# A loop over batch rows, written out for all 16 rows

## What is computed

```python
# attention: each block of 128 queries sees its own, the block before and the block after,
# and within these only keys at a distance of at most 128
scores = einsum('bhnqd,bhnkd->bhnqk', qb, kwin) / 16      # masked to -1e30
out = einsum('bhnqk,bhnkd->bhnqd', softmax(scores), vwin) @ Wout + bout
x = layernorm(x + out)
# FFN with both weight matrices quantised to -1, 0, 1
h = relu(x @ Wq1.T + b1)
x = layernorm(x + h @ Wq2.T + b2)
```

## Time and profile before

| | |
|---|---|
| three runs | 1191.0, 1196.81, 1200.02 us (median 1196.81) |
| the profiled execution | 1195.88 us, of it 1194.1 us from first to last instruction |
| PE busy | 1055.2 us, 88% |
| DVE, ACT, POOL busy | 72%, 51%, 44% |
| mean granted TensorE clock | 0.934 of full speed |
| instructions executed | 28091 |

### The profile page before, as it was taken

The page is one execution under the profiler, slowest core; times in us unless marked ns, Lnnn a source line. Parts: engine busy times, 40 slices in busy tenths (PEclk is TensorE's granted clock), DMA queues, the critical chain, the costliest instruction groups (busy, mean ns, idle before and its releaser), DMA issues.

```text
span 1194.1 us, 28091 instructions
## 1 busy us (share of the span) xinstructions
PE 1055.2 (88%) x8132; PEld 772.8 (65%) x8132; DVE 859.5 (72%) x2934; ACT 613.2 (51%) x1258; POOL 521.0 (44%) x824
## 2 busy tenths in 40 slices
PE   4788899998989899898989999898989989897966
PEld 3454676766667576666767676666757666675755
DVE  3875787778787777778777777878777777877233
ACT  4154564555455564655456465545556465554421
POOL 2124353544545444453535354454544446354330
PEclk9576899999999999999999999999999999897879
DMA  5835244434244443444244443425444344422000
GB/s 167 108 51 94 29 82 81 68 68 71 55 77 65 80 71 75 59 81 67 48 80 80 81 65 68 71 53 78 65 80 71 75 59 71 61 50 55 11 9 18
DMA packets 56924, 80.51 MB, mean 67 GB/s; under 512 B 7729, under 2 KB 27697, under 8 KB 56882
## 3 DMA queue, kind: packets, MB, share of 16 engines
q1 hardware_dynamic: 56882, 80.00, 39.8%
HBM read 20.19 MB, written 8.39 MB: 24 GB/s over the span
## 4 chain that ended last, share of the span: by engine, by line
PE 74%; DVE 12%; issue 7%; POOL 2%; ACT 2%; DMA 1%; DVEq 1%; SPq 0%; POOLq 0%; ACTq 0%
PE shared L498 18%; PE st_a L473 12%; PE shared L517 12%; PE shared L596 10%; PE shared L609 9%; PE st_b L473 4%; DVE mx L830 4%; PE shared L592 3%; PE shared L578 2%; DVE rmax L830 2%; DVE x L922 2%; POOL ln_rstd L1036 1%; PE mx L489 1%; DVE oT_lo L877 1%; PE shared L557 1%
## 5 line engine op out<-in xcount | busy, mean ns | idle before, releaser
L830 DVE CUSTOM_DVE_ANT_0 mx<-mx,band 128x384 f32<-128x384 f32 (+1 forms) x1024 | 480.7, 514 | 197.3 <-PE mx L489 194.2
L684 ACT ACTIVATE probs<-st_a 128x384 f32<-128x384 f32 (+1 forms) x384 | 201.9, 526 | 367.8 <-PE st_a L473 362.2
L489 PE MATMUL mx<-k_stack,q_stack 48*128 48x384 f32 (+1 forms) x1024 | 272.6, 368 | 7.0 <-DMA k_stack<-qk_lo 4.0
L997 POOL TENSOR_SCALAR_AFFINE_SELECT probs<-probs 128x512 f32<-128x512 f32 (+1 forms) x256 | 129.7, 530 | 318.6 <-ACT probs L684 318.6
L684 ACT ACTIVATE probs<-st_b 128x384 f32<-128x384 f32 (+1 forms) x384 | 200.8, 523 | 0.2 <-PE st_b L473 0.2
L473 PE MATMUL st_a<-q_stack,k_stack 50*128 50x384 f32 (+1 forms) x512 | 185.1, 403 | 3.1 <-ACT probs L684 2.4
L489 PEld LDWEIGHTS mx<-k_stack,q_stack 48*128 48x128 f32 x1024 | 164.7, 199 | 12.4 <-DVE rmax L830 7.8
L517 PE MATMUL shared<-probs,v_aug 128*32 128x384 f32 (+1 forms) x2048 | 161.6, 446 | 0.8 <-DVE x L922 0.8
L473 PEld LDWEIGHTS st_a<-q_stack,k_stack 50*128 50x128 f32 x512 | 89.7, 196 | 101.6 <-issue 63.0
L830 DVE DVE_READ_ACCUMULATOR2_ANT rmax<- 128x1 f32 x1024 | 143.7, 140 | 0.0
L596 PE MATMUL shared<-x1T_hi,w1q 128*128 128x256 f32 x512 | 143.5, 296 | 0.0
(11 more groups left out here) (107 smaller groups left out, 1962.0 us busy)
## 6 DMA issues: line engine op xcount, KB each, us to landing
q_stack<-qk_hi SPq DMA_DIRECT2D x128, 128.0 KB, 4.3
k_stack<-qk_hi SPq DMA_DIRECT2D x128, 128.0 KB, 5.3
x_raw<-in_xT SPq DMA_DIRECT2D x16, 512.0 KB, 5.0
q_stack<-qk_lo SPq DMA_DIRECT2D x64, 128.0 KB, 3.9
k_stack<-qk_lo SPq DMA_DIRECT2D x64, 128.0 KB, 5.4
y<-in_x SPq DMA_DIRECT2D x16, 512.0 KB, 6.0
out<-x SPq DMA_DIRECT2D x32, 256.0 KB, 2.1
probs<-in_w2T SPq DMA_DIRECT2D x1, 1024.0 KB, 10.6
```

The costliest lines, as they stand in the source:

```text
L489: mm = pe.matmul(PMX[i % N_MAX][:, col:col + n], SQ[rows, hd, W * m:W * m + W], SK[rows, hd, k0:k0 + n], start=True, stop=True)
L684: act.activation(PR[:, v % 2, g // 2, lo:lo + n], PST[i % 2][:, 0:n], ACT.Exp, scale=SCALE) \
L830: mx = dve.tensor_tensor_reduce(ps, ps, band, 1.0, -3e38, ALU.add, ALU.max, RMAX[:, g, m:m + 1])
L997: pool.affine_select(out=pr_before, in_=pr_before, compare_op=ALU.is_ge, fill=0.0, base=0, pattern=[[0, n], [1, W]], channel_multiplier=-1)
```

## The change

The loop is gone: `steps` calls the step function with a plain number for each of the 19 steps on each engine. Every semaphore is then waited for with a constant, every address is a constant, `in_register` is removed, and so are the waits on `s_const` that went with it, in the steps that were written out before as well. The order of the work, the tiles, the transfers and the semaphores' counts stay as they were.

```diff
-def steps(eng, step):
-
-    for at in (-2, -1, 0, 1):
-        step(at, at)
-    with eng.Fori(2, B - 2) as b:
-        step(b, None)
-    for at in (B - 2, B - 1, B):
-        step(at, at)
-
-
-def in_register(eng, count):
-
-
-    if isinstance(count, int):
-        return count
-    reg = eng.alloc_register()
-    eng.reg_mov(reg, count)
-    return eng.snap(reg)
+def steps(step):
+
+    for row in range(-2, B + 1):
+        step(row, row)
...
-                    sp.dma_start(XRAW[:, :, :], xT[bass.ds(b + 2, 1)].rearrange("a (c p) t -> p (a c) t", p=P)) \
+                    sp.dma_start(XRAW[:, :, :], xT[b + 2:b + 3].rearrange("a (c p) t -> p (a c) t", p=P)) \
...
-                    count = in_register(dve, 4 * r + v)
-                    dve.wait_ge(s_const, CONSTANTS)
-                    dve.wait_ge(s_nm, count)
-                count = in_register(dve, 12 * (4 * r + v) + i + 1)
-                dve.wait_ge(s_const, CONSTANTS)
-                dve.wait_ge(s_mxf, count)
+                    dve.wait_ge(s_nm, 4 * r + v)
+                dve.wait_ge(s_mxf, 12 * (4 * r + v) + i + 1)
...
-                        count = in_register(dve, 4 * r + 1 + t)
-                        dve.wait_ge(s_const, CONSTANTS)
-                        dve.wait_ge(s_st1, count)
+                        dve.wait_ge(s_st1, 4 * r + 1 + t)
...
-                count = in_register(pool, 3 * (16 * b + 4 * v + g) + 3)
-                pool.wait_ge(s_const, CONSTANTS)
-                pool.wait_ge(s_exp, count)
+                pool.wait_ge(s_exp, 3 * (16 * b + 4 * v + g) + 3)
...
-                    count = in_register(pool, 4 * r + 4)
-                    pool.wait_ge(s_const, CONSTANTS)
-                    pool.wait_ge(s_mv1, count)
+                    pool.wait_ge(s_mv1, 4 * r + 4)
```

More of the change, by code:

```diff
@@ L416, in step @@
                             sp.wait_ge(s_x1, 4 * b)
-                        sp.dma_start(Y[:, :, :], x[bass.ds(b, 1)].rearrange("a (t p) d -> p (a t) d", p=P)) \
+                        sp.dma_start(Y[:, :, :], x[b:b + 1].rearrange("a (t p) d -> p (a t) d", p=P)) \
                             .then_inc(s_xr, 16)
@@ L430, in store @@
                 sp.wait_ge(s_o, 4 * (b - 1) + 2 * hf + 2)
-                sp.dma_start(out[bass.ds(b - 1, 1), 256 * hf:256 * hf + 256].rearrange("a (t p) d -> p (a t) d", p=P),
+                sp.dma_start(out[b - 1:b, 256 * hf:256 * hf + 256].rearrange("a (t p) d -> p (a t) d", p=P),
                              X1[:, 2 * hf:2 * hf + 2, :]).then_inc(s_od, 16)
-            steps(sp, step)
+            steps(step)
             sp.wait_ge(s_od, 32 * B)
@@ L644, in step @@
                 assert at is not None or reader == entry
-            steps(pe, step)
+            steps(step)
         @block.scalar
@@ L771, in step @@
                             side_work(v, step, b, *row, at)
-            steps(act, step)
+            steps(step)
         @block.vector
@@ L931, in side_work @@
                     for t in ((t - 1, t) if t % 2 else ()):
-                        count = in_register(dve, 4 * r + 1 + t)
-                        dve.wait_ge(s_const, CONSTANTS)
-                        dve.wait_ge(s_st2, count)
+                        dve.wait_ge(s_st2, 4 * r + 1 + t)
                         dve.bn_aggr(MV2[:, t, :], ST[:, t, :]).then_inc(s_mv2, 1)
@@ L961, in step @@
                                 side_work(v, what, b, *row, at)
-            steps(dve, step)
+            steps(step)
         @block.gpsimd
@@ L1005, in v_in_place @@
             def v_in_place(r, v, first):
-                count = in_register(pool, 4 * (r - 1) + v + 1)
-                made = in_register(pool, 2 * r + 2)
-                pool.wait_ge(s_const, CONSTANTS)
-                pool.wait_ge(s_v, made)
+                pool.wait_ge(s_v, 2 * r + 2)
                 if not first:
-                    pool.wait_ge(s_pvf, count)
+                    pool.wait_ge(s_pvf, 4 * (r - 1) + v + 1)
                 pool.tensor_copy(VAUG[:, v, :, :, 0:DH],
@@ L1047, in side_work @@
                     two = slice(2 * hf, 2 * hf + 2)
-                    count = in_register(pool, 4 * r + 2 * hf + 2)
-                    pool.wait_ge(s_const, CONSTANTS)
-                    pool.wait_ge(s_mv2, count)
+                    pool.wait_ge(s_mv2, 4 * r + 2 * hf + 2)
                     pool.tensor_scalar(VE[:, two], MV2[:, two, 1], 1.0, EPS, ALU.mult, ALU.add).then_inc(s_ve, 1)
@@ L1055, in side_work @@
                         return
-                    count = in_register(pool, 2 * r + hf + 1)
-                    pool.wait_ge(s_const, CONSTANTS)
-                    pool.wait_ge(s_rs2, count)
+                    pool.wait_ge(s_rs2, 2 * r + hf + 1)
                     for t in (2 * hf, 2 * hf + 1):
@@ L1078, in step @@
                             side_work(v, step, b, *row, at)
-            steps(pool, step)
+            steps(step)
 def kernel(L0_attn_x, L0_attn_Wqkv, L0_attn_bqkv, L0_attn_Wout, L0_attn_bout, L0_ffn_W1, L0_ffn_b1,
```

## The result

The changed kernel took 1186.47 us (median of 16 runs, 1184.61 to 1188.29) against 1196.69 (16 runs, 1187.5 to 1203.94): ratio 0.9922, interval 0.9902 to 0.9942. Two later sets on other occasions gave 1187.87 (ratio 0.9976, 0.9952 to 1.0) and 1186.62 (0.9952, 0.9926 to 0.9978). The changed kernel hardly moves between sets; the kernel before does (medians 1189.6 to 1196.7 in five sets), so the gain is 0.2 to 0.8%, about half a per cent. Ratios leave out three executions more than 1.5% above the fastest of their kernel (two of e1, one of e13), and are not those of the medians. The forecast was no change, 1195.7 with a range of 1188 to 1201.

What follows compares the result with a forecast made beforehand. TensorE, busy 88%, was taken as the bound, with clock slow stretches setting the step. Twelve steps at 68.27 gave 0, an earlier last stall -0.2: 1195.88 - 0.2 = 1195.7 us, range 1188 to 1201.

Steps and rivals of the forecast that it cites:

- the spacing of the slow stretches: Steps 2 to 13: half-speed clock stretches stay 68.27 us apart and hold the mean step there, so 0 gained.
- the 0.1 that the prediction allowed: Its test for steps 2 to 13: wrong if their mean leaves 68.27 us by more than 0.1.
- the 0.32 that it worked with: Per loop step, ahead of the x1 transposes: 0.19 + 0.01 + 0.12 us saved against a written-out step.
- kept gain: Rival: slow stretches do not follow, each loop step keeps 0.32 us, 3.8 in all, 1192.0 us; chance 0.22.
- no slow stretch: Rival: the stall shifts to where the clock does not fall, 24.2 us gained, 1171.7 us; chance 0.06.
- code arrives late: Rival: 48 more code fetches hold TensorE's queue, up to +41 us, 1237 us; chance 0.05.
- the other edits: Removed s_const waits in all steps, constant transfer addresses and added code: each taken as 0.
- a bound of 1.7 us: Removed s_const waits: at most 0.12 us in each of 14 steps; taken as 0.
- the model of an unrolled step: Written-out step 14, laid beside loop step 7 on TensorE: 68.32 us against 68.25.
- 0.12 of the 0.32: Stretch before the first x1 transpose: 2.92 us in the loop, 2.80 written out, put down to POOL's registers.
- the prediction's own sign on start and end: It would be wrong if start and end changed by more than the runs' spread, 1191.0 to 1200.02 us.

Runs made afterwards that it cites:

- e1: Kernel before with loop and registers kept, waits on s_const removed from the written-out steps alone: 1187.2 us, ratio 0.9975.
- e13: Repeat in a later set of the kernel before with its loop, waits on s_const removed from the written-out steps alone: 1189.12 us, ratio 0.9978.
- e2: Changed (unrolled) kernel with all nine waits on s_const put back: 1194.23 us, ratio 1.0024 to the kernel before.
- e15: Changed kernel with the nine waits on s_const put back in steps -2 to 13 alone: 1188.74 us.
- e5: The changed kernel itself, run again in the second set: 1187.87 us, ratio 0.9976 to the kernel before.
- e16: The changed kernel itself, run again in the fourth set as its measure: 1186.62 us, ratio 0.9952 to the kernel before.
- e14: Changed kernel with the nine waits on s_const put back in steps 14, 15 and 16 alone: 1192.05 us.
- e6: Changed kernel with one of the nine waits on s_const put back, that ahead of each row maximum: 1187.77 us.
- e4: Changed kernel with the first norm's power replaced by a product, so x1 is not normalised rightly and the stall is shorter: 1160.4 us, ratio 0.9738.
- e11: Changed kernel with x1 tile 2 moved from ACT to DVE and the first norm's statistics one row maximum earlier on DVE: 1148.53 us, ratio 0.9654.
- e7: Changed kernel with projection (qk, 3) moved ahead of two x1 transposes to fill the stall: 1281.1 us, ratio 1.075.

## Why the prediction was wrong

**What held.** The forecast for the 12 loop steps was a mean of 68.27 us, the spacing of the slow stretches, whatever a step saves. It nearly did: middles of 958.66 to 959.87 us in all eight traces of unrolled kernels with the old norm chain, e2 and e15 with 0.3 us less work in a step than the loop, e5 and e16 with 0.85 less. Taken alone, steps 2 to 13 have means of 68.24 to 68.28 in six of them. In the other two, 68.12 in the first trace of the changed kernel and 68.14 in e14, they leave 68.27 by a little more than the 0.1 that the prediction allowed. e2 and e15, which save the 0.32 that it worked with, also have its pattern: slow stretches of 3.4 and 6.8 us in mixture and steps from 67.9 to 68.5. Elsewhere the pattern differs and the mean hardly does. In e14, whose middle has the changed kernel's instructions, three steps take 68.75, 70.08 and 66.00 us; the x1 transposes of steps 5, 6, 7 and 8:

```profile
410.35 0.45 PE L568 MATMUL shared<-identity,x 128*128 128x128 f32 x1 [1.47 <-ACT x L731]
479.10 0.45 PE L568 MATMUL shared<-identity,x 128*128 128x128 f32 x1 [1.46 <-ACT x L731]
549.18 0.30 PE L568 MATMUL shared<-identity,x 128*128 128x128 f32 x1 [1.47 <-ACT x L731]
615.18 0.45 PE L568 MATMUL shared<-identity,x 128*128 128x128 f32 x1 [1.46 <-ACT x L731]
```

That is 204.83 us for three, 68.28 a step. The step of 66.00 has no slow stretch at all, and the one before it has one of 10.2 us. So a missing slow stretch, too, was given back. The rivals "kept gain" (67.93 a step), "no slow stretch" (as a gain) and "code arrives late" did not happen. The code of 12 more steps, 45 more pieces on queue 8, held up nothing that the middles show. The Trainium skill (Runtime: NRT & Kernel Launch, Instruction fetch mechanics) says of a long program that its fetch is mostly hidden; the traces agree, with middles of 959 us either way.

68.27 us is not the only length that steps keep, though. In e1's trace the steps of the same loop alternate between some 69.5 and 70.5 us from step 2 to step 13, a mean of 69.98, and never come to 68.27. The prediction had no such case, and what decides between the two is open.

**The step that failed: the other edits.** I put the waits on s_const at 0, with a bound of 1.7 us and none against the start and end, since "only waits go that were long satisfied". The wait is satisfied, but it is not free: with it the wait that matters becomes an instruction of its own ahead of the operation. The trace of before had the row, which I had not set beside the change:

```profile
L825 DVEq EVENT_SEMAPHORE  x768: 21/21/136, 35.2 to 1101.1; - x192
```

What it costs is seen where DVE waits for TensorE. Before, then after: the last matmul that the first maximum of a quad reads, and that maximum.

```profile
529.05 0.28 PE L489 MATMUL mx<-k_stack,q_stack 48*128 48x256 f32 x1
...
529.51 0.43 DVE L830 CUSTOM_DVE_ANT_0 mx<-mx,band 128x256 f32<-128x256 f32 x1 [1.72 <-PE mx L489]
```

```profile
526.40 0.27 PE L475 MATMUL mx<-k_stack,q_stack 48*128 48x256 f32 x1
...
526.75 0.43 DVE L812 CUSTOM_DVE_ANT_0 mx<-mx,band 128x256 f32<-128x256 f32 x1 [2.05 <-PE mx L475]
```

0.46 us from matmul to maximum became 0.35. It is the wait and not the loop's registers: e6, unrolled and with this one wait back, has 0.45 at the same place.

```profile
526.56 0.27 PE L475 MATMUL mx<-k_stack,q_stack 48*128 48x256 f32 x1
...
527.01 0.43 DVE L813 CUSTOM_DVE_ANT_0 mx<-mx,band 128x256 f32<-128x256 f32 x1 [2.13 <-PE mx L475]
```

e6's total and end also say that this 0.1 us alone is hidden; it counts in the end only together with the eight other waits. Step 14, which I took as the model of an unrolled step, still had these waits, so the model saved 0.32 us a step where the real one saves 0.85. The cause that I gave for 0.12 of the 0.32, registers between POOL's small operations, isn't in the rows either: from the start of L1034 to that of L1040 the loop's step took 1.62 us and step 14 took 1.68. It is the last of them, L1040, that took 0.29 us in the loop and 0.20 outside.

**And its place.** I wrote that the change could touch only the loop steps, though the same nine waits go from the written-out ones. In the middle the error cost nothing, as all savings are given back there. In the last steps the savings were kept: the waits put back in steps 14 to 16 alone cost 5.7 us there (125.89 against 120.23) and 5.4 us of the median, where I had put nothing. I read it so, that there is no next step to keep to. End 125.83 and 125.82 us with the waits and the loop, 126.36 with the waits alone, 125.89 with the waits in steps 14 to 16; 120.27, 120.24, 120.23, 119.97 and 119.22 without them there. Of the 5.6 us, 4.9 is TensorE's busy time (96.31 to 91.38), the same matmuls at a higher mean clock: the end had 42.2 us at half speed before and has 32.5 after. TensorE's idle time there fell by 0.6 us alone. Why shorter waits left the clock up for longer was not separated. Both traces of the kernel before are of executions near 1195.5 us; those near 1187, of which every set has some, were not traced, and whether their end is 125.8 too isn't shown.

**The loop's share.** Looped kernels have middles of 959.36, 962.69 and 962.55 us, unrolled ones 958.66 to 959.87. By these traces writing the loop out gives 0.5 to 4 us, not by cheaper steps but because the loop's steps, 68.25 us of own length, have no room under the 68.27 and come slowly to their place from a bad start. That is argued from three traces of loops, not tested by itself, and the medians don't settle it: e13, loop without the waits in its written-out steps, is 2.0 us above e16, within their spread, while e2, the kernel before without its loop, is 4.7 above the kernel before. What is shown is the waits' part; whether the loop itself had one is open.

**The range.** Its lower end, 1188, left out a gain in start and end, and was missed by 1.5 us. The 7.5 us by which start and end are shorter in the trace lie within the 9 us between the runs shown then, so the prediction's own sign on start and end would not have caught the error; the runs with the waits put back did.

## What to carry to other kernels

Before costing a removed wait at nothing, look in the trace for the instruction that it makes: a second wait, even one long satisfied, can push the real one into an instruction of its own, ahead of every operation that then waits. Where a kernel loses TensorE's clock once a step, look at the spacing of the slow stretches first; savings elsewhere may come back in them, while a slightly shorter idle just ahead of them can be worth several times its length (3.1 us for 0.86 in four steps of e4). And cut the span at the first and last steps, and check what the change touches there: a saving that the middle gives back may be kept in the end.

## What the runs showed of the hardware

The granted clock set the length of the step. With an idle of 1.46 us before the x1 transposes, and 1.41 before the u transpose just ahead, it fell to half for 6.8 us in nearly every step of the changed kernel, and the steps came to 68.2 to 68.3 us; e14's same steps had 6.8 us, 10.2 us and none in turn, with nearly the same mean. With 0.60 us (e4) it stayed at full speed in four steps and these took 65.13. Moving two small pieces of work (e11: one x1 tile from ACT to DVE, the first norm's statistics earlier on DVE) was worth 38 us in 1187, where all the removed register work and waits were worth 4 to 10. The opposite, a well-meant filling of one idle that opened another of 5 us (e7), cost 93 us.
